# First stage of a three-stage transformer kernel: biases loaded in one piece, TensorE's products regrouped, VectorE's loop unrolled

## The chip, the cores and the metric

The kernel runs on one NeuronCore of a Trainium2 chip. The metric is device time in microseconds of one execution; before the change the median of three runs is 1351.59 us (1350.39 to 1354.27). One more execution was profiled, and its trace is what the rows below come from.

## The reference

Images of 64 x 3 x 128 x 128 are cut into 64 patches of 768 numbers. A first block mixes over the batch with weights of its own for each patch n, a linear chain of five products follows, then a recurrent attention layer and a feed-forward layer. The change touches only the first block:

```python
flat = x.reshape(64, 3, 8, 16, 8, 16).transpose(0, 2, 4, 1, 3, 5).reshape(64, 64, 768)
q = einsum('bnf,nfd->bnd', flat, Wq) + bq        # Wq, Wk, Wv: (64, 768, 192); bq, bk, bv: (64, 192)
k = einsum('bnf,nfd->bnd', flat, Wk) + bk
v = einsum('bnf,nfd->bnd', flat, Wv) + bv
scores = einsum('bnd,cnd->nbc', q, k) / sqrt(192)
attn = einsum('nbc,cnd->bnd', softmax(scores), v)
att = layernorm(attn) * ln_g + ln_b + flat @ p1_w + p1_b
h = chain(att) + att @ p2_w + p2_b               # chain: w0..w4 with biases, linear
h = softmax(h, axis=2)
h = h + attention(layernorm(h)); h = h + ffn(layernorm(h))
```

## The kernel before

Everything is fp32. The five products of the chain and p2 are linear, so the kernel first multiplies them into one 192 x 192 matrix and a bias (`weff`); that is the opening, 0 to about 68 us, TensorE work on `bt` and `chain_w`. Then comes the **first stage**: 32 pairs of patches, one pair per step. For a pair, 128 partitions hold 64 batch rows of each of two patches. A step costs three weight loads of 1152 KB each (Wq, Wk, Wv of two patches) and one of 384 KB (x). The second stage (from about 440 us on) is the recurrent attention and the feed-forward part; no line of it is touched.

Each engine has a program of its own, written out by hand, and the engines meet by semaphores; so the order of the lines in a `step_b` of each engine is the order in which the engine works. A step s works on three pairs at once: `t` = s is new (its products with the weights), `a` = s - 1 is in the middle (scores and softmax), `c2` = s - 2 is old (attention times v, layer norm, projection, softmax). On **TensorE** (`pe`) the pieces of a step have these names below:

- **qk**: `qk_chunk` 0 to 5, 12 products of 64 columns of the array by 384; two products on the two halves of the array run side by side.
- **v**: `v_chunk`, 12 products of 64 columns by 192. **p1**: `p1_chunk`, 6 products of 128 columns by 192.
- **tqk**: four transposes of q and k of pair a. **scores**: four small products of 64 columns.
- **pt**: the transpose of the softmax of pair a. **attn**: its product with v.
- **attT**: two transposes of `att` of pair c2. **proj**: two products with `weff`.

An fp32 product is two records in the trace. Before the change the order is: qk 0-1, tqk, qk 2-5, scores, attT, v 0-2, proj, v 3-5, p1 0-2, pt, p1 3-5, attn. ScalarE copies results out of PSUM: q and k (L832), `attT` (L838, L840), the two exponentials of the scores (L851), that of the last softmax (L857), pt into `probsT` (L863), v (L868). VectorE adds the biases (L1212 for bv, L1224 for bq and bk), makes the layer norm with GpSimd's power between (L1215 to L1238), the maxima (L1241, L1248) and the last scaling (L1262). In steps 2 to 5 VectorE also centres and splits the weights of the second stage (`centre_weights`, `split_weights`), in order behind its own part of the step.

**SyncE** issues all DMAs, in one queue. `load_pair(t)` waits until the buffers of pair t - 2 are free: Wq and Wk for `qk_mm`, Wv for `v_mm`, x for `qkv_done` (p1 done). `load_biases` issues three small DMAs for each pair: 3 KB of bq and bk, and twice 48 KB of bv, each row of bv repeated over 64 partitions. TensorE's step t waits for all four loads of its pair (`wx_in`, 64 counts) before its first qk.

Of the kernel before, what the change touches and what calls it, by code (L numbers as in the profile page):

```python
# [19 lines left out]
ALU = mybir.AluOpType  # L20
# [38 lines left out]
 bias_in0 bias_in1 h_out0 h_out1 qkv_done qk_mm v_mm qk_copied v_copied tqk_mm qkT_ready scores_mm rmax_ready  # L59
# [44 lines left out]
def build(nc, d, out):  # L104

    with ExitStack() as ctx:
# [75 lines left out]
        qk_bias = [part("first", HALF, 2, 4) for _ in range(2)]  # L182
        bv = [part("first", P, ATT) for _ in range(2)]
# [25 lines left out]

        bt = [part("first", P, HC, ATT + 1) for _ in range(2)]  # L210
# [80 lines left out]
        def _(sp):  # L291
# [9 lines left out]
                     (p1w[:, :, :], d["p1_w"])]  # L301
# [39 lines left out]
            load_biases(Step(0, 0))  # L341
# [12 lines left out]

            def step_b(it, u):
                t = Step(it, u)
                if t.inside(PAIRS):
                    load_pair(t)
                t = Step(it, u, 1)
                if t.inside(PAIRS):  # L360
                    load_biases(t)
                c2 = Step(it, u, 4)
                if c2.after(0):
                    store_h(c2)
# [71 lines left out]
        def _(pe):  # L436
# [30 lines left out]
            pe.wait_ge(S["par_in"], 20 * 16)  # L467
# [12 lines left out]
            def step_b(it, u):  # L480
                t, a, c2 = Step(it, u), Step(it, u, 1), Step(it, u, 2)
                new, mid, old = t.inside(PAIRS), a.inside(PAIRS), c2.inside(PAIRS)

                def qk_chunk(c_):
                    for e in range(2):
                        last = mm(PS[64 * e:64 * e + 64, 0, 0:2 * ATT], xt[t.par][:, c_, 64 * e:64 * e + 64],
                                  wt[t.par][:, e, 0:2, c_, :], c_ == 0, c_ == CH - 1)
                    if c_ == CH - 1:
                        last.then_inc(S["qk_mm"], 1)

                def v_chunk(c_):
                    for e in range(2):
                        last = mm(PS[64 * e:64 * e + 64, 1 + t.par, 0:ATT], xt[t.par][:, c_, 64 * e:64 * e + 64],
                                  wt[t.par][:, e, 2, c_, :], c_ == 0, c_ == CH - 1)
                    if c_ == CH - 1:
                        last.then_inc(S["v_mm"], 1)

                def p1_chunk(c_):
                    last = mm(PS[:, 1 + t.par, ATT:2 * ATT], xt[t.par][:, c_, :], p1w[:, c_, :], c_ == 0, c_ == CH - 1)
                    if c_ == CH - 1:  # L500
                        last.then_inc(S["qkv_done"], 1)

                if new:
                    pe.wait_ge(S[f"wx_in{t.par}"], (t.half + 1) * 64)
                    if t.after(1):
                        pe.wait_ge(S["qk_copied"], t.n)
                    qk_chunk(0)
                    qk_chunk(1)
                if mid:
                    pe.wait_ge(S["qk_copied"], a.n + 1)  # L510
                    if a.after(1):
                        pe.wait_ge(S["qkT_ready"], a.n)
                    for k in range(4):
                        last = nc.tensor.transpose(PS[0:HALF, 3, k * P:(k + 1) * P], qk[:, k * HALF:(k + 1) * HALF], ident)  # L514
                    last.then_inc(S["tqk_mm"], 1)
                if new:
                    for c_ in range(2, CH):
                        qk_chunk(c_)
                if mid:
                    pe.wait_ge(S["qkT_ready"], a.n + 1)  # L520
                    if a.after(1):
                        pe.wait_ge(S["expP_ready"], 2 * a.n)
                    for e in range(2):
                        for k in range(2):
                            last = mm(PS[64 * e:64 * e + 64, 4, 0:64], qkT[:, k, 64 * e:64 * e + 64],
                                      qkT[:, 2 + k, 64 * e:64 * e + 64], k == 0, k == 1)
                    last.then_inc(S["scores_mm"], 1)
                if old:
                    pe.wait_ge(S["att_ready"], c2.n + 1)
                    if c2.after(1):  # L530
                        pe.wait_ge(S["zexp_ready"], c2.n)
                    nc.tensor.transpose(PS[0:HALF, 7, 0:P], att[:, 0:HALF], ident)  # L532
                    nc.tensor.transpose(PS[0:HALF, 7, P:2 * P], att[:, HALF:ATT], ident).then_inc(S["attT_mm"], 1)
                if new:
                    if t.after(2):
                        pe.wait_ge(S["v_copied"], t.n - 1)
                        pe.wait_ge(S["att_ready"], t.n - 1)
                    for c_ in range(3):
                        v_chunk(c_)
                if old:  # L540
                    pe.wait_ge(S["attT_copied"], 2 * c2.n + 2)
                    mm(PS[:, 7, 2 * P:2 * P + ATT], attT1[:, :], weff1[:, :], True, False)
                    mm(PS[:, 7, 2 * P:2 * P + ATT], attT2[:, :], weff2[:, :], False, True).then_inc(S["proj_mm"], 1)
                if new:
                    for c_ in range(3, CH):
                        v_chunk(c_)
                    for c_ in range(3):
                        p1_chunk(c_)
                if mid:
                    pe.wait_ge(S["expP_ready"], 2 * a.n + 2)  # L550
                    if a.after(1):
                        pe.wait_ge(S["pt_copied"], a.n)
                    nc.tensor.transpose(PS[:, 5, 0:P], probs[:, :], ident).then_inc(S["pt_mm"], 1)
                if new:
                    for c_ in range(3, CH):
                        p1_chunk(c_)
                if mid:
                    pe.wait_ge(S["pt_copied"], a.n + 1)
                    pe.wait_ge(S["v_copied"], a.n + 1)
                    if a.after(1):  # L560
                        pe.wait_ge(S["attn_ready"], a.n)
                    mm(PS[:, 6, 0:ATT], probsT[:, :], v[a.par][:, :]).then_inc(S["attn_mm"], 1)
# [258 lines left out]
        def _(act):  # L821
            act.wait_ge(S["par_in"], 20 * 16)
# [3 lines left out]
            def step_b(it, u):  # L826
                t, a, c2 = Step(it, u), Step(it, u, 1), Step(it, u, 2)
                if t.inside(PAIRS):
                    act.wait_ge(S["qk_mm"], t.n + 1)
                    if t.after(1):  # L830
                        act.wait_ge(S["tqk_mm"], t.n)
                    act.activation(qk[:, :], PS[:, 0, 0:2 * ATT], ACT.Copy).then_inc(S["qk_copied"], 1)  # L832
                if c2.inside(PAIRS):
# [25 lines left out]
                if a.inside(PAIRS):  # L859
# [3 lines left out]
                    act.activation(probsT[:, :], PS[:, 5, 0:P], ACT.Copy).then_inc(S["pt_copied"], 1)  # L863
                if t.inside(PAIRS):
                    act.wait_ge(S["qkv_done"], t.n + 1)
                    if t.after(2):
                        act.wait_ge(S["attn_mm"], t.n - 1)
                    act.activation(v[t.par][:, :], PS[:, 1 + t.par, 0:ATT], ACT.Copy).then_inc(S["v_copied"], 1)  # L868
# [263 lines left out]
        def _(dve):  # L1132
            dve.wait_ge(S["par_in"], 20 * 16)
# [70 lines left out]
            def step_b(it, u):  # L1204
                a, c2 = Step(it, u, 1), Step(it, u, 2)
                mid, old = a.inside(PAIRS), c2.inside(PAIRS)
                if old:

                    dve.wait_ge(S["attn_mm"], c2.n + 1)
                    dve.wait_ge(S[f"bias_in{c2.par}"], (c2.half + 1) * 48)  # L1210
                    dve.wait_ge(S["prec_ready"], c2.n + 1)
                    dve.scalar_tensor_tensor(out=attn[:, :], in0=PS[:, 6, 0:ATT], scalar=prob_rec[:, :], in1=bv[c2.par][:, :],  # L1212
# [6 lines left out]
                if mid:  # L1219
                    dve.wait_ge(S["tqk_mm"], a.n + 1)  # L1220
                    dve.wait_ge(S[f"bias_in{a.par}"], (a.half + 1) * 48)
                    if a.after(1):
# [3 lines left out]
                                      qk_bias[a.par].rearrange("p e k -> p k e").unsqueeze(3).to_broadcast([HALF, 4, 2, 64]),  # L1226
                                      ALU.add).then_inc(S["qkT_ready"], 1)
                if old:
# [9 lines left out]
                    dve.tensor_tensor(att[:, :], PS[:, 1 + c2.par, ATT:2 * ATT], bhatg[:, :], ALU.add).then_inc(S["att_ready"], 1)  # L1238
# [31 lines left out]
            pipeline(dve, PAIRS, 4, step_b_and_weights)  # L1270
# [258 lines left out]
def host_layout(i):  # L1529
# [10 lines left out]
    d["bqk"] = np.concatenate([halves(a["tok_bq"]), halves(a["tok_bk"])], axis=2).transpose(0, 3, 1, 2)  # L1540
    d["bv"] = a["tok_bv"].reshape(PAIRS, 2, 1, ATT)
# [51 lines left out]
```

## Time and profile before

| | us |
|---|---|
| median of three runs | 1351.59 |
| profiled execution, whole | 1347.21 |
| its span in the trace | 1345.2 |
| opening (until the first qk) | 67.87 |
| first stage, first qk to last result of VectorE | 67.87 to 437.89 |

The span is what the trace shows from the first instruction to the last; 2.0 us lie around it. Times in rows count from the span's start. In the timelines a row is a run of like instructions: its start, its busy time, the engine, the line, what it writes and reads, how many, and in brackets how long the engine was idle before it and what ended that.

### The profile page before, as it was taken

What the parts mean: (1) busy time and instruction counts of PE and PEld (TensorE: products, weight loads), DVE (VectorE), ACT (ScalarE), POOL (GpSimd) and SP (SyncE); (2) the same over time, 40 slices, a digit from 0 to 9 for tenths busy, and PEclk for the clock granted to TensorE, in tenths of its full rate; (3) what the DMA queues carried; (4) which work ended last, traced back from release to release, by engine and by line L of the source; (5) the groups of instructions that cost most, each with busy time, mean ns of one, the idle gap of its engine ahead of it and who ended that gap; (6) DMA issues with size and microseconds to landing.
All of it is one profiled execution on the core that took longest, in us unless ns stands there. A gap on an engine that the chain in (4) does not pass through costs nothing.

```text
span 1345.2 us, 44929 instructions
## 1 busy us (share of the span) xinstructions
PE 1231.8 (92%) x17572; PEld 988.4 (73%) x17572; DVE 858.4 (64%) x2184; ACT 614.7 (46%) x1539; POOL 542.5 (40%) x689
## 2 busy tenths in 40 slices
PE   5898999999997579999999999999999999999975
PEld 5865666666664468888888888888888887888774
DVE  0137433333333368878887888888788878888762
ACT  0012222222222355656665666656566656665532
POOL 0000000000000356566646665665566466656631
PEclk8999999999998689999999999999999999999987
DMA  9888999999991012112212221221122122211210
GB/s 326 300 327 325 381 379 372 374 375 373 376 376 37 18 22 50 32 37 50 38 35 39 46 38 35 40 47 35 36 45 44 32 38 50 38 35 35 47 32 15
DMA packets 219992, 179.22 MB, mean 133 GB/s; under 512 B 164342, under 2 KB 189881, under 8 KB 219321
## 3 DMA queue, kind: packets, MB, share of 16 engines
q1 hardware_dynamic: 219818, 176.79, 41.2%
q8 instruction: 122, 2.00, 0.6%
q14 instruction: 52, 0.43, 0.1%
HBM read 154.72 MB, written 22.02 MB: 131 GB/s over the span
## 4 chain that ended last, share of the span: by engine, by line
PE 32%; issue 29%; POOL 27%; DVE 6%; SPq 2%; DMA 2%; ACT 1%; POOLq 0%; DVEq 0%; ACTq 0%
PE PS L438 28%; POOL region L1110 9%; POOL region L1093 5%; POOL region L1098 3%; POOL region L1076 2%; POOL region L1104 2%; POOL region L1088 1%; PE PS L514 1%; SPq L308 1%; POOL region L1083 1%; POOL region L1060 1%; SPq L398 1%; PE PS L692 1%; PE PS L532 1%; PE PS L599 1%
## 5 line engine op out<-in xcount | busy, mean ns | idle before, releaser
L438 PE MATMUL PS<-region 64*64 64x64 f32 (+6 forms) x5864 | 351.6, 286 | 19.9 <-DVE region L1158 12.7
L438 PEld LDWEIGHTS PS<-region 64*64 64x64 f32 (+3 forms) x5864 | 230.1, 139 | 114.9 <-issue 105.0
L1110 POOL TENSOR_TENSOR region<-region,powers 128x12 f32<-128x12 f32 x96 | 224.2, 2336 | 7.5
L905 ACT ACTIVATE region<-PS 128x512 f32<-128x512 f32 (+1 forms) x192 | 93.3, 486 | 187.1 <-PE PS L438 187.1
L1039 POOL TENSOR_TENSOR region<-region,powers 128x1 f32<-128x1 f32 x32 | 6.1, 189 | 404.2 <-DVE region L1218 404.2
L692 PEld LDWEIGHTS PS<-region 64*64 64x64 f32 x4608 | 145.6, 138 | 22.9 <-issue 18.9
L692 PE MATMUL PS<-region 64*64 64x64 f32 x4608 | 158.4, 223 | 1.4 <-ACT region L938 1.4
L438 PE MATMUL PS<-cw_hi,xr_hi 128*128 128x512 f32 (+3 forms) x384 | 148.5, 387 | 1.9 <-ACT region L905 1.4
L438 PE MATMUL PS<-cw_lo,xr_hi 128*128 128x512 f32 (+3 forms) x384 | 130.6, 340 | 0.0
L438 PE MATMUL PS<-cw_hi,xr_lo 128*128 128x512 f32 (+3 forms) x384 | 130.2, 339 | 0.0
L1351 DVE TENSOR_TENSOR region<-region 128x768 f32<-128x768 f32 x96 | 102.8, 1072 | 39.2 <-POOL region L1110 38.9
L832 ACT ACTIVATE region<-PS 128x384 f32<-128x384 f32 x32 | 15.7, 491 | 192.5 <-PE PS L438 192.5
L1057 POOL TENSOR_TENSOR region<-region,powers 128x1 f32<-128x1 f32 x32 | 6.1, 190 | 228.5 <-DVE region L1442 228.5
L1340 DVE TENSOR_REDUCE region<-region 128x12 f32<-128x768 f32 x96 | 90.7, 945 | 6.6 <-ACT region L910 6.3
L889 ACT ACTIVATE region<-PS,vecs 128x256 f32<-128x256 f32 (+1 forms) x128 | 75.7, 669 | 41.4 <-PE PS L648 41.3
L682 PE MATMUL PS<-region 64*64 64x64 f32 x3072 | 62.0, 226 | 29.4 <-issue 22.3
L682 PEld LDWEIGHTS PS<-region 64*64 64x64 f32 x3072 | 54.3, 138 | 46.8 <-issue 46.8
L1093 POOL TENSOR_TENSOR region<-region,powers 128x12 f32<-128x12 f32 x32 | 72.9, 2277 | 26.9 <-DVE region L1410 26.8
L438 PEld LDWEIGHTS PS<-cw_hi,xr_hi 128*128 128x128 f32 (+1 forms) x384 | 73.0, 190 | 14.5 <-ACT region L905 2.2
L910 ACT ACTIVATE region<-region 128x768 f32<-128x768 f32 x96 | 81.1, 845 | 2.8
L438 PEld LDWEIGHTS PS<-cw_hi,xr_lo 128*128 128x128 f32 (+1 forms) x384 | 73.0, 190 | 8.9
L438 PEld LDWEIGHTS PS<-cw_lo,xr_hi 128*128 128x128 f32 (+1 forms) x384 | 74.0, 193 | 4.6
(170 smaller groups left out, 2280.0 us busy)
## 6 DMA issues: line engine op xcount, KB each, us to landing
region<-in_Wq SPq DMA_DIRECT2D x32, 1152.0 KB, 6.3
region<-in_Wk SPq DMA_DIRECT2D x32, 1152.0 KB, 8.6
region<-in_Wv SPq DMA_DIRECT2D x32, 1152.0 KB, 7.8
region<-in_x SPq DMA_DIRECT2D x32, 384.0 KB, 7.4
n_scratch<-region SPq DMA_DIRECT2D x64, 192.0 KB, 3.3
region<-h_scratch SPq DMA_DIRECT2D x64, 96.0 KB, 2.0
region<-in_w SPq DMA_DIRECT2D x2, 2304.0 KB, 13.2
region<-i_scratch SPq DMA_DIRECT2D x256, 12.0 KB, 1.8
```

Of the source, the lines that this page charges most:

```text
L438: return nc.tensor.matmul(dst, lhsT, rhs, start=first, stop=last)
L682: done = nc.tensor.matmul(dst(slice(to, to + 64), h), lhsT[rows, h, :], rhs(rows, h), start=h < 2, stop=stop, skip_group_check=True)
L692: done = nc.tensor.matmul(dst(rows, h), eT[rows, h, :], rhs(rows, h), start=start and h == odd, stop=stop, skip_group_check=True)
L889: act.activation(kqT[:, pairs, m, :], PS[:, bank, at:at + n * P].rearrange("p (a b) -> p a b", a=n), ACT.Identity, scale=(lnk_g, lnq_g)[m] ...
L905: act.activation(raw[:, col:col + width], PS[:, PIECE_BANK[i], 0:width], ACT.Copy).then_inc(S["raw_ready"], 1)
L910: act.activation(sq[:, m * KD:(m + 1) * KD], raw[:, m * KD:(m + 1) * KD], ACT.Square, scale=HD ** -0.5).then_inc(S["sq_ready"], 1)
L1076: pool.tensor_tensor(tr[:, 4:5], tr[:, 3:4], root[:, 0:1], ALU.pow).then_inc(S["f_rstd"], 1)
L1093: pool.tensor_tensor(norm[:, 1, :], norm[:, 0, :], square_root[:, 0:HEADS], ALU.pow).then_inc(S["n1"], 1)
L1098: pool.tensor_tensor(nscale[:, :, :], mask_n.unsqueeze(1).to_broadcast([P, HEADS, SEQ]), norm[:, 5, :].unsqueeze(2).to_broadcast([P, HEADS ...
L1110: pool.tensor_tensor(rs[:, cols], rs_var[:, cols], root[:, cols], ALU.pow).then_inc(S["rs_ready"], 1)
L1340: dve.tensor_reduce(ssq[:, m * HEADS:(m + 1) * HEADS], sq.rearrange("p (g d) -> p g d", d=HD) [:, m * HEADS:(m + 1) * HEADS, :], AX, ALU.a ...
L1351: dve.tensor_tensor(dst.rearrange("p (g d) -> p g d", d=HD), raw[:, m * KD:(m + 1) * KD].rearrange("p (g d) -> p g d", d=HD), rs[:, m * HE ...
```

## The change

Three parts. (1) All biases are loaded once. bq and bk of all pairs come in one DMA of 96 partitions among the small parameters. bv of all pairs goes, in two DMAs of 64 partitions by 6144 numbers, over the place of `bt` and `chain_w[0]`, which are the buffers of the opening; SyncE therefore waits for the last product of the opening (`eff_mm`) ahead of them. The three small DMAs for each pair are gone. (2) TensorE's step has a new order: attn of c2, tqk, qk 0-5, v 0-5, attT, scores, p1 0-2, proj, p1 3-5, pt. v has one PSUM bank instead of two, p1 two banks of its own, pt lies in the bank of the scores; ScalarE copies v right behind q and k. (3) VectorE's loop of 34 steps is written out (it was a hardware loop with 8 steps ahead and 4 behind).

```diff
-        qk_bias = [part("first", HALF, 2, 4) for _ in range(2)]
-        bv = [part("first", P, ATT) for _ in range(2)]
+        qk_bias = part("first", HALF, PAIRS, 8)
...
+        bv = region[:, used["first"]:used["first"] + PAIRS * ATT].rearrange("p (m f) -> p m f", m=PAIRS)
         bt = [part("first", P, HC, ATT + 1) for _ in range(2)]
...
-                     (p1w[:, :, :], d["p1_w"])]
+                     (qk_bias[:, :, :], d["bqk"]), (p1w[:, :, :], d["p1_w"])]
...
-            def load_biases(t):
-                if t.after(2):
-                    sp.wait_ge(S["attn_ready"], t.n - 1)
-                    settled(sp)
-                sp.dma_start(qk_bias[t.par][:, :, :], d["bqk"][t.n]).then_inc(S[f"bias_in{t.par}"], 16)
-                for e in range(2):
-                    sp.dma_start(bv[t.par][e * 64:e * 64 + 64, :], d["bv"][t.n, e].to_broadcast([64, ATT]))\
-                      .then_inc(S[f"bias_in{t.par}"], 16)
...
+            sp.wait_ge(S["eff_mm"], 1)
+            settled(sp)
+            for e in range(2):
+                sp.dma_start(bv[64 * e:64 * e + 64, :, :], d["bv"][e].to_broadcast([64, PAIRS, ATT])).then_inc(S["bias_in"], 16)
...
-                if new:
-                    pe.wait_ge(S[f"wx_in{t.par}"], (t.half + 1) * 64)
-                    if t.after(1):
-                        pe.wait_ge(S["qk_copied"], t.n)
-                    qk_chunk(0)
-                    qk_chunk(1)
+                if old:
+                    pe.wait_ge(S["pt_copied"], c2.n + 1)
+                    pe.wait_ge(S["v_copied"], c2.n + 1)
+                    if c2.after(1):
+                        pe.wait_ge(S["attn_ready"], c2.n)
+                    mm(PS[:, 6, 0:ATT], probsT[:, :], v[c2.par][:, :]).then_inc(S["attn_mm"], 1)
...
-            pipeline(dve, PAIRS, 4, step_b_and_weights)
+            for s in range(PAIRS + 2):
+                step_b_and_weights(s // 2, s % 2)
```

How the instructions stand on TensorE: first the end of one step of the loop and the start of the next. L438 is the helper `mm` (L430 after the change); 64x384 is qk, 64x192 is v, `p1w` is p1, L553 (L546) is pt, 128x192 from `region` alone is attn, L514 (L506) is tqk. Before:

```order
L438 MATMUL PS<-region 64x192 x6
L438 MATMUL PS<-p1w,region 128x192 x3
L550 REGISTER_ALU
L553 MATMUL PS<-cst,region 128x128 [waits pt_copied,expP_ready]
L438 MATMUL PS<-p1w,region 128x192 x3
L438 MATMUL PS<-region 128x192 [waits attn_ready,v_copied,pt_copied]
L506 REGISTER_ALU [waits wx_in1]
L438 MATMUL PS<-region 64x384 [waits qk_copied]
```

After the change:

```order
L430 MATMUL PS<-p1w,region 128x192 x3
L545 ISA
L546 MATMUL PS<-cst,region 128x128 [waits expP_ready]
L430 MATMUL PS<-region 128x192 [waits attn_ready,v_copied,pt_copied]
L502 REGISTER_ALU
L506 MATMUL PS<-cst,region 96x128 [waits qkT_ready,qk_copied]
L506 MATMUL PS<-cst,region 96x128 x3
L430 MATMUL PS<-region 64x384 [waits v_copied,qk_copied,wx_in1]
L430 MATMUL PS<-region 64x384 x11
L430 MATMUL PS<-region 64x192 x12
```

The three products of p1 that stood between pt and attn now stand ahead of pt, and attn follows pt with nothing between. The middle of a step, again on TensorE; 64x64 is scores, L532 and L533 (L521, L522) are attT, `weff` is proj. Before:

```order
L438 MATMUL PS<-region 64x384 x8
L522 REGISTER_ALU [waits qkT_ready]
L438 MATMUL PS<-region 64x64 [waits expP_ready]
L438 MATMUL PS<-region 64x64 x3
L531 REGISTER_ALU [waits att_ready]
L532 MATMUL PS<-cst,region 96x128 [waits zexp_ready]
L533 MATMUL PS<-cst,region 96x128
L438 MATMUL PS<-region 64x192 [waits att_ready,v_copied]
L438 MATMUL PS<-region 64x192 x5
L541 ISA
L438 MATMUL PS<-weff,region 128x192 [waits attT_copied]
L438 MATMUL PS<-weff,region 128x192
```

After the change:

```order
L430 MATMUL PS<-region 64x384 x11
L430 MATMUL PS<-region 64x192 x12
L521 MATMUL PS<-cst,region 96x128 [waits zexp_ready,att_ready]
L522 MATMUL PS<-cst,region 96x128
L430 MATMUL PS<-region 64x64 [waits pt_copied,qkT_ready]
L430 MATMUL PS<-region 64x64 x3
L430 MATMUL PS<-p1w,region 128x192 [waits att_ready]
L430 MATMUL PS<-p1w,region 128x192 x2
L430 MATMUL PS<-weff,region 128x192 [waits attT_copied]
L430 MATMUL PS<-weff,region 128x192
L430 MATMUL PS<-p1w,region 128x192 x3
```

The v products stand in one run behind qk, ahead of attT and scores, and proj stands between two runs of p1. The third place is SyncE's queue at the end of the opening, from the last parameters of the second stage to the load of pair 2. Before:

```order
L353 DMA wo<-in_WoT 128x1152
L353 DMA ffn1a<-in_ffn1T 128x128
L353 DMA ffn1b<-in_ffn1T 64x128
L325 DMA region<-in_Wq 128x2x1152 [waits qk_mm]
L325 DMA region<-in_Wk 128x2x1152
L325 DMA region<-in_Wv 128x2x1152 [waits v_mm]
L330 DMA region<-in_x 128x768 [waits qkv_done]
L314 DMA region<-in_bqk 96x8
L316 DMA region<-in_bv 64x192 x2
```

After the change:

```order
L343 DMA ffn1a<-in_ffn1T 128x128
L343 DMA ffn1b<-in_ffn1T 64x128
L348 DMA region<-in_bv 64x6144 [waits eff_mm]
L348 DMA region<-in_bv 64x6144
L316 DMA region<-in_Wq 128x2x1152 [waits qk_mm]
L316 DMA region<-in_Wk 128x2x1152
L316 DMA region<-in_Wv 128x2x1152 [waits v_mm]
L321 DMA region<-in_x 128x768 [waits qkv_done]
```

Ahead of the load of pair 2 there are now two DMAs of 64 partitions by 6144 numbers and the wait for `eff_mm`.

## Rows read from the trace of the kernel before

**Rows 1.** A stretch of the steady first stage: busy times, granted clock, DMA

```profile
core 0: us, PE busy (x) PEld busy (x) DVE busy (x) ACT busy (x) POOL busy (x), PEclk, DMA share, GB/s
...
370.00:403.00 33.00, 33.00 (x244) 21.03 (x241) 12.39 (x43) 8.75 (x33) 2.21 (x6) 1.00 0.99 375
```

**Rows 2.** Timeline of one step of the steady loop

```profile
202.28 0.64 PE L514 MATMUL PS<-cst,region 128*96 128x128 f32 x4
...
203.23 0.14 PEld L438 LDWEIGHTS PS<-region 128*64 128x64 f32 x2 [0.18 <-issue]
203.55 0.14 PEld L438 LDWEIGHTS PS<-region 128*64 128x64 f32 x2 [0.18 <-issue]
...
206.22 1.20 PE L438 MATMUL PS<-region 128*64 128x192 f32 x12
...
207.34 0.92 PE L438 MATMUL PS<-weff,region 96*128 96x192 f32 x4
...
210.40 0.27 PE L553 MATMUL PS<-cst,region 128*128 128x128 f32 x1
...
210.51 1.14 PE L438 MATMUL PS<-p1w,region 128*128 128x192 f32 x6
210.71 0.28 ACT L863 ACTIVATE region<-PS 128x128 f32<-128x128 f32 x1 [1.32 <-PE PS L553]
...
211.49 1.93 PE L438 MATMUL PS<-region 128*128 128x192 f32 x10
...
213.35 0.64 PE L514 MATMUL PS<-cst,region 128*96 128x128 f32 x4
```

**Rows 3.** Timeline of the last steps: an attn that waits for its copy

```profile
428.57 0.27 ACT L863 ACTIVATE region<-PS 128x128 f32<-128x128 f32 x1
...
428.89 0.50 PEld L438 LDWEIGHTS PS<-region 128*128 128x128 f32 x2 [1.42 <-ACT region L863]
```

**Rows 4.** Timeline of step 4: VectorE behind the centring of weights

```profile
94.69 1.36 DVE L1186 TENSOR_SCALAR region<-region 49x2304 f32<-49x2304 f32 x1
...
101.36 0.41 DVE L1212 SCALAR_TENSOR_TENSOR region<-PS,region 128x192 f32<-128x192 f32 x1
...
104.61 0.32 PE L532 MATMUL PS<-cst,region 128*96 128x128 f32 x1 [0.93 <-DVE region L1238]
```

**Rows 5.** TensorE's waits from 85 to 135 us: us in total, times, longest

```profile
PE PS L438 <- DVE region L1224: 2.1, 2, 1.8
PE PS L532 <- DVE region L1238: 1.8, 2, 0.9
```

**Rows 6.** Timeline: last product of the opening, first qk, pair 2

```profile
64.13 0.35 DVE L1161 TENSOR_TENSOR weff<-PS,p2a 96x192 f32<-96x192 f32 x1 [4.31 <-PE PS L438]
...
67.87 6.04 PE L438 MATMUL PS<-region 128*64 128x384 f32 x48 [2.47 <-DVE ffn_bias L1176]
...
72.04 0.38 SPq L325 DMA_DIRECT2D region<-in_Wq  x1
...
85.55 0.20 PEld L438 LDWEIGHTS PS<-region 128*64 128x64 f32 x4 [0.23 <-issue]
```

**Rows 7.** Load of x for pair 2 (issued at 76.1 us)

```profile
DMA to landing us min/median/max: 9.0/9.0/9.0
```

**Rows 8.** Stretches of the opening, columns as in rows 1

```profile
17.00:19.50 2.50, 2.50 (x18) 2.50 (x17) 0.00 (x0) 0.00 (x0) 0.00 (x0) 1.00 0.99 69
53.00:61.00 8.00, 6.25 (x39) 5.97 (x38) 1.53 (x2) 0.00 (x0) 0.00 (x0) 1.00 1.01 189
64.00:72.00 8.00, 5.53 (x37) 3.47 (x37) 3.02 (x10) 0.00 (x0) 0.00 (x0) 1.00 0.04 14
74.00:80.00 6.00, 6.00 (x38) 3.56 (x40) 0.69 (x1) 0.33 (x1) 0.00 (x0) 1.00 1.00 409
```

**Rows 9.** Timeline: TensorE starts again in the opening

```profile
29.69 3.56 PE L438 MATMUL PS<-region 128*128 128x193 f32 x10 [9.24 <-DVE region L1158]
```

**Rows 10.** The stretch around that start, columns as in rows 1

```profile
24.90:35.10 10.20, 5.41 (x17) 5.44 (x18) 2.91 (x11) 0.22 (x1) 0.00 (x0) 0.50 1.03 409
```

More of the change, by code:

```diff
@@ L516, in step_b @@
                 if new:
-                    for c_ in range(2, CH):
-                        qk_chunk(c_)
[L519 to L527, printed above, removed]
+                    pe.wait_ge(S[f"wx_in{t.par}"], (t.half + 1) * 64)
+                    if t.after(1):
+                        pe.wait_ge(S["qk_copied"], t.n)
+                        pe.wait_ge(S["v_copied"], t.n)
+                    for c_ in range(CH):
+                        qk_chunk(c_)
+                    for c_ in range(CH):
+                        v_chunk(c_)
                 if old:
@@ L533, in step_b @@
                     nc.tensor.transpose(PS[0:HALF, 7, P:2 * P], att[:, HALF:ATT], ident).then_inc(S["attT_mm"], 1)
+                if mid:
+                    pe.wait_ge(S["qkT_ready"], a.n + 1)
+                    if a.after(1):
+                        pe.wait_ge(S["pt_copied"], a.n)
+                    for e in range(2):
+                        for k in range(2):
+                            last = mm(PS[64 * e:64 * e + 64, 4, 0:64], qkT[:, k, 64 * e:64 * e + 64],
+                                      qkT[:, 2 + k, 64 * e:64 * e + 64], k == 0, k == 1)
+                    last.then_inc(S["scores_mm"], 1)
                 if new:
                     if t.after(2):
-                        pe.wait_ge(S["v_copied"], t.n - 1)
                         pe.wait_ge(S["att_ready"], t.n - 1)
                     for c_ in range(3):
-                        v_chunk(c_)
+                        p1_chunk(c_)
                 if old:
@@ L550, in step_b @@
                     pe.wait_ge(S["expP_ready"], 2 * a.n + 2)
[L551 to L562, printed above, removed]
+                    nc.tensor.transpose(PS[:, 4, P:2 * P], probs[:, :], ident).then_inc(S["pt_mm"], 1)
             for s in range(2):
@@ L862, in step_b @@
                         act.wait_ge(S["attn_mm"], a.n)
[L863 to L868, printed above, removed]
+                    act.activation(probsT[:, :], PS[:, 4, P:2 * P], ACT.Copy).then_inc(S["pt_copied"], 1)
             pipeline(act, PAIRS, 2, step_b)
@@ L1209, in step_b @@
                     dve.wait_ge(S["attn_mm"], c2.n + 1)
-                    dve.wait_ge(S[f"bias_in{c2.par}"], (c2.half + 1) * 48)
+                    dve.wait_ge(S["bias_in"], 32)
                     dve.wait_ge(S["prec_ready"], c2.n + 1)
-                    dve.scalar_tensor_tensor(out=attn[:, :], in0=PS[:, 6, 0:ATT], scalar=prob_rec[:, :], in1=bv[c2.par][:, :],
+                    dve.scalar_tensor_tensor(out=attn[:, :], in0=PS[:, 6, 0:ATT], scalar=prob_rec[:, :], in1=bv[:, c2.n, :],
                                              op0=ALU.mult, op1=ALU.add).then_inc(S["attn_ready"], 1)
```

31 lines of the change are left out of this document (14 added, 17 removed).

## The prediction

> **What bounds the kernel now.** I looked at stretches of the first stage first, since only that stage is changed. From 134 to 403 us TensorE has no idle time at the full clock, and DMA shows 0.99 of its time busy at 375 GB/s [rows 1]. Two resources seem full, so the question is which one waits. The view of waits names nothing that TensorE waited for between 134 and 403 us, no DMA in particular. DMA runs at 409 GB/s when it has work [rows 8], and a step needs 3.93 MB of weights and x plus some 0.2 MB: 4.1 MB / 409 GB/s = 10.1 us of a step of 213.35 - 202.28 = 11.07 us [rows 2]. So TensorE is the bound in the steady part, and DMA has 1 us to spare in each step. VectorE is busy 12.39 of 33 us [rows 1]: writing its loop out gives nothing by itself.
>
> Two places are not steady. In steps 3 to 5 TensorE waits 2.1 + 1.8 = 3.9 us for VectorE [rows 5], which stands behind the second stage's weights [rows 4]. And the load of pair 2 comes just in time: its x is issued at 76.1 and lands 9.0 us later, at 85.1 [rows 7], and TensorE's first qk of that pair starts at 85.55 [rows 6]. Whatever delays that load by more than about half a microsecond stops TensorE, and nothing makes it up later, since every later step is TensorE's.
>
> **The change part by part.**
>
> *Fewer changes of shape.* The trace gives the pure price of each run. qk: two loads of weights start 0.32 apart (203.23, 203.55), 12 times 3.84 us. A record of p1 takes (211.49 - 210.51) / 6 = 0.163, 12 times 1.95. v is half as wide as qk, 12 x 0.163 = 1.95. attn and proj, 6 x 0.163 = 0.98. Seven transposes at 210.51 - 210.40 = 0.11 make 0.77, the four pairs of scores 0.21 by their width. The sum is 9.70, against 11.07 [rows 2]: 1.37 us go into changes between products on half of the array's columns (64) and those on all of them. There are eight in a step: to tqk and back, scores to attT, attT to v, v to proj and back, v to p1, attn to qk. That is 0.17 each. The v run of 206.22 to 207.34 has 1.12 for six products of 0.163, so 0.14 for one change. The new order has four: tqk to qk, v to attT, attT to scores, scores to p1. It saves four, 0.56 to 0.68 us a step; I take 0.62.
>
> *attn directly behind pt.* Between them lies a trip through ScalarE: pt goes to `probsT` and attn reads it. Before, three products of p1 hid it. Now nothing does. pt starts at 210.40, ScalarE's copy at 210.71 and takes 0.28 [rows 2]; in the last steps a copy ended at 428.84 and attn's weights began to load at 428.89 [rows 3]. From pt's start to attn's that is 0.31 + 0.28 + 0.05 = 0.64, of which 0.11 is pt itself: 0.53 idle. Behind it attn's weights no longer load under a running product; that is a start like one after a change of shape, 0.10. In every second step the wait stands on a register instruction at the loop's head, 0.05 on average. Sum 0.67 us. Is ScalarE free for the copy? The last softmax's exponential follows proj; proj stands six p1 records and pt's trip, about 1.4 us, ahead, about what the maximum, its negation and the exponential need. I count no more for it; if the copy is late, each 0.1 us costs 3 us over the stage.
>
> Net in a steady step 0.67 - 0.62 = +0.05; over 30 steps +1.5 us. The bounds: 0.53 - 0.68 = -0.15 gives -4.5 us, and 0.78 (the trip and 0.1 of a late copy) - 0.56 = +0.22 gives +6.6 us. The last trip stands in the drain, where nothing is saved: +0.5.
>
> *Steps 2 to 5.* VectorE's work on the weights takes 101.36 - 94.69 = 6.67 us in step 2, and 3.25 more pass until attT can start (104.61) [rows 4]. In the new order TensorE has 0.43 (attn) + 0.58 (tqk) + 3.84 + 1.95 = 6.8 us of work between attn and attT. I let VectorE end its own part when attn starts, because its last results hang on proj, which is now 1.4 us ahead of that. Then attT waits 6.67 + 3.25 - 6.8 = 3.1 us, against 1.8 + 0.9 before [rows 5]: +0.4. The three other blocks are shorter; with the same shift of 0.3 each, the four cost +1.3 us. What waits behind attT is all of the rest of the step, so this is on the path.
>
> *v copied earlier, banks, SyncE's small DMAs.* The earlier copy waits for v and is needed a step later; the small DMAs (99 KB a step) relieve DMA, which has spare time, and SyncE. 0 here. If the steps became 1 us shorter, DMA would be next.
>
> *The single load of bv.* This is the term that decides. It is 2 x 64 x 6144 x 4 B = 3.15 MB, as much as was loaded in pieces, but all ahead of pair 2. SyncE issues it when the opening's last product is through, 64.1 [rows 6]. DMA is indeed idle then, 0.04 of 64 to 72 us [rows 8], and the load of pair 2 is issued at 72.04 [rows 6]. With 1.5 us from issue to flow, at 409 GB/s the 3.15 MB would end at 73.3 and hide. But each of the two DMAs goes to one half of the partitions. The same form stands in the trace: from 53 to 61 us the weights of 64 and of 49 partitions flow, DMA is 1.01 busy, and it moves 189 GB/s [rows 8]. At that rate bv takes 16.6 us and ends at 65.7 + 16.6 = 82.3. The Trainium skill says why (SBUF — State Buffer, section "Door 1: The DMA port swizzle"): partitions 0 to 63 reach only 8 of 16 ports, at best about 218 GB/s, and two DMAs to the two halves do not add up. By its figure, which is an estimate from that page, bv takes 14.4 us; the stretch at 189 GB/s agrees with the rule.
>
> The weights of pair 2 stand behind it in the queue. 3.93 MB at 409 GB/s are 9.6 us, and 1 us goes by until the slowest of the queues is through (before: 72.04 + 1.5 to 85.1 is 11.6, with the start from an idle queue). I take a rate between 189 and half of 409, which ends bv at 81.3: x lands at 91.9. TensorE comes to the first qk of pair 2 at 85.55 + 0.67 (trip) + 0.58 (tqk now stands ahead) - 0.2 (changes saved) = 86.6. It idles **5.3 us**; bounds 4.3 and 6.3.
>
> *The clock.* That idle time has a price of its own. In the opening TensorE stopped for 9.24 us up to 29.69 [rows 9], and its granted clock was 0.50, the lower of the two levels (1.2 GHz), from 24.9 to 35.1 [rows 10]: it fell 4.4 us after the engine had stopped and came back 5.4 us after it had started, at a loss of 2.7. An idle time of 5.3 us is near the 4.4; I count half, +1.3.
>
> **Sum.** 1.5 + 0.5 + 1.3 + 5.3 + 1.3 = +9.9 us on the profiled 1347.2, so 1357 for a profiled execution, and 1351.6 + 9.9 = 1361.5, about **1361 us**, for the median, which stood 4.4 above the profiled one. The likeliest case's own range: 1355 to 1368.
>
> **The rivals.**
> - *bv flows at the full rate and hides.* For: engines may drift apart, so that both halves are written at once. Against: 189 GB/s in the like stretch. Then 5.3 and 1.3 fall away, +3.3: 1355 us. Chance 13%.
> - *bv is held up at its source.* All 64 partitions read the same row. For: from 17 to 19.5 us four small loads of one row to 128 partitions flowed, DMA 0.99 busy, 69 GB/s [rows 8]. Against: the pieces in the steady stage do the same and cost no wait. At 69 GB/s bv takes 45.6 us, x of pair 2 lands near 122, TensorE idles 35: 1351.6 + 3.3 + 35 + 2.7 = 1393 us. Chance 12%.
> - *The new order wins.* Place: from pt to attn in each step. If TensorE did not lose the trip (the next run of weights and tqk going on in its shadow), a step would be 11.07 - 0.62 = 10.45, 18.6 us less over 30; with the load of pair 2 late as above, 1351.6 - 18.6 + 8.4 = 1341 us. It decides from a loss under 0.2 us per step on, where the saving pays for the late load too. Against it stands the order: attn is in front of tqk in the same queue. Chance 11%.
>
> **How the numbers follow.** A measurement tells this kernel from no change beyond about 0.3%, 4 us. The likeliest case has 64%, and is slower by more than that in nine of ten; the second rival is slower; the first is mostly within 4 us, the third faster. That makes slower 0.74, the same 0.14, faster 0.12. The range leaves out the second rival and most of the third: 1349 to 1371.
>
> **What the profile would show.** Right: about 65.7 to 81 us at about 200 GB/s; x of pair 2 landing near 92; TensorE idle some 5 us before its third run of qk, at the lower clock for a few us behind it; a steady step of 11.0 to 11.2 us with one idle time of about 0.5 us, ended by L851, in each. Wrong: a step under 10.8 (the trip is not lost), bv done by 74 (full rate) or after 90 (source), or a wait of attn much over 0.6 us, which would mean that ScalarE is not free and would move the result up by 3 us for each 0.1.

## The result

The kernel after the change takes **1359.39 us** (median of 7 executions, 1354.75 to 1363.51), the kernel before, timed beside it, 1350.39 (7 executions, 1346.89 to 1354.27). The ratio is **1.0073**, its 95% interval 1.0056 to 1.009: slower by 7.6 to 12.2 us. The prediction had 1361, a range of 1349 to 1371, and slower at 0.74. In two of the experiments below one execution lay far off (2355.40 us in e3, 3701.27 in e11) and is left out of the ratio.

The two profiled executions lie further apart than the medians, 1360.7 against 1345.2 us of span. Where these 15.5 us arise:

| place | before | after | after is behind by |
|---|---|---|---|
| first qk of pair 0 | 67.87 | 67.62 | -0.25 |
| first qk of pair 2 | 85.55 | 91.46 | 5.9 |
| tqk of the last pair | 422.03 | 433.10 | 11.1 |
| first product of the second stage | 446.30 | 458.44 | 12.1 |
| end of the span | 1345.2 | 1360.7 | 15.5 |

The last 3.4 us arise in the second stage, whose code is the same (granted clock 0.97 before, 0.96 after, over that stretch), and are no part of the change. The first 5.9 are the place that the prediction named. By the issue of x for pair 5 the kernel is 10.2 behind (110.61 before, 120.76 after), and from there to the last pair only 1 us is added. TensorE's timeline of the changed kernel there (columns as in [rows 2]):

```profile
86.17 0.27 PE L546 MATMUL PS<-cst,region 128*128 128x128 f32 x1
86.90 0.59 PE L430 MATMUL PS<-region 128*128 128x192 f32 x2 [0.45 <-ACT region L851]
87.32 0.60 PE L506 MATMUL PS<-cst,region 128*96 128x128 f32 x4
91.46 0.91 PE L430 MATMUL PS<-region 128*64 128x384 f32 x2 [3.54 <-DMA region<-in_x]
```

The last row is the first qk of pair 2, with 3.54 us of idle time ended by x. [rows 6] show 85.55 for it (its weights' load) and no wait. SyncE's queue of the same kernel shows why x is late:

```profile
63.92 1.11 SPq L348 DMA_DIRECT2D region<-in_bv  x2
73.48 0.39 SPq L316 DMA_DIRECT2D region<-in_Wq  x1
...
77.58 0.34 SPq L321 DMA_DIRECT2D region<-in_x  x1
```

and the views of the lines L348 (both DMAs of bv) and L321 (x of pair 2) give the times from issue to landing:

```profile
L348 SPq DMA_DIRECT2D region<-in_bv x2: 471/534/597, 63.9 to 64.4; - x2
...
DMA to landing us min/median/max: 9.7/13.1/16.6
...
L321 SPq DMA_DIRECT2D region<-in_x x1: 340/340/340, 77.6 to 77.6; - x1
...
DMA to landing us min/median/max: 13.8/13.8/13.8
```

bv is issued at 63.9 and 64.4 and lands at 73.6 and 81.0; x of pair 2 lands at 77.6 + 13.8 = 91.4, where [rows 7] have 9.0 us for it. Stretches of the changed kernel (columns as in [rows 1]):

```profile
66.00:72.00 6.00, 4.38 (x18) 2.20 (x20) 1.30 (x5) 0.00 (x0) 0.00 (x0) 0.75 0.96 197
74.00:80.00 6.00, 6.00 (x48) 4.43 (x45) 0.69 (x1) 0.33 (x1) 0.00 (x0) 1.00 0.93 189
91.00:98.00 7.00, 6.54 (x28) 2.74 (x30) 0.00 (x0) 0.03 (x1) 0.00 (x0) 0.62 1.02 421
113.50:120.00 6.50, 5.93 (x25) 5.46 (x26) 1.44 (x7) 1.93 (x8) 0.00 (x0) 0.50 0.92 376
370.00:403.00 33.00, 31.82 (x245) 21.83 (x243) 12.19 (x43) 9.06 (x33) 2.21 (x6) 1.00 0.96 363
```

While bv flows, DMA is 0.93 to 0.96 busy and moves 189 to 197 GB/s, half of the 409 that [rows 8] have for weights: 3.15 MB at 193 GB/s are 16.3 us. Behind the idle time the granted clock is at the lower level (0.50, 1.2 GHz) for most of 91 to 98 (0.62 on average), and once more from 113.5 to 120 (0.50). In a view of TensorE alone qk and v of pair 2 are one row, and it takes 8.40 us where the like row of pair 0 has 6.04 in [rows 6]:

```profile
91.46 8.40 PE L430 MATMUL PS<-region 128*64 128x384 f32 x48 [3.54 <-DMA region<-in_x]
```

In the steady stretch TensorE, which had 33.00 of 33 us in [rows 1], has 31.82: there is now an idle time in each step. TensorE's waits from 62 to 145 us, and from 145 to 405 (columns as in [rows 5]):

```profile
PE PS L521 <- DVE region L1220: 4.8, 2, 3.2
PE PS L430 <- DMA region<-in_x: 3.5, 1, 3.5
...
PE PS L430 <- ACT region L851: 2.1, 5, 0.5
...
PE PS L430 <- ACT region L851: 9.8, 24, 0.4
```

One steady step of TensorE and of ScalarE's copy:

```profile
210.83 0.27 PE L546 MATMUL PS<-cst,region 128*128 128x128 f32 x1
211.55 0.59 PE L430 MATMUL PS<-region 128*128 128x192 f32 x2 [0.45 <-ACT region L851]
...
221.93 0.27 PE L546 MATMUL PS<-cst,region 128*128 128x128 f32 x1
...
211.14 0.28 ACT L851 ACTIVATE region<-PS 128x128 f32<-128x128 f32 x1
```

pt starts at 210.83, the copy at 211.14, attn at 211.55: the trip takes 0.72 us, and 0.45 of it show as idle (0.64 and 0.37 in every second step). Yet the step is no longer than before: SyncE issues x alternately 11.01 and 11.11 us apart, 11.06 on average, against 11.07 [rows 2].

### The profile page after: what moved, and what is told of

It is laid out like the page before. It is cut to its first block, busy times and chain, and to the rows that moved or that the text cites. A ratio compares the mean times of both kernels' runs of the same rounds, so it can differ in the third digit from the quotient of the medians.

```text
span 1360.7 us, 44475 instructions
## 1 busy us (share of the span) xinstructions
PE 1230.5 (90%) x17572; PEld 1003.1 (74%) x17572; DVE 857.5 (63%) x2184; ACT 618.2 (45%) x1539; POOL 542.4 (40%) x689
## 4 chain that ended last, share of the span: by engine, by line
issue 31%; POOL 28%; PE 27%; DVE 7%; DMA 3%; SPq 2%; ACT 2%; POOLq 0%; DVEq 0%; ACTq 0%
PE PS L430 24%; POOL region L1093 9%; POOL region L1076 5%; POOL region L1081 3%; POOL region L1087 2%; POOL region L1059 2%; POOL region L1071 1%; POOL region L1043 1%; SPq L308 1%; POOL region L1066 1%; DMA region<-in_x 1%; DVE region L1230 1%; PE PS L506 1%; PE PS L521 1%; ACT region L851 1%
## 5 line engine op out<-in xcount | busy, mean ns | idle before, releaser
L430 PE MATMUL PS<-region 64*64 64x64 f32 (+6 forms) x5864 | 346.5, 287 | 32.3 <-ACT region L851 13.7
L430 PEld LDWEIGHTS PS<-region 64*64 64x64 f32 (+3 forms) x5864 | 235.1, 140 | 137.1 <-issue 114.3
L430 PE MATMUL PS<-cw_hi,xr_hi 128*128 128x512 f32 (+3 forms) x384 | 149.5, 389 | 1.9 <-ACT region L888 1.4
L430 PE MATMUL PS<-cw_lo,xr_hi 128*128 128x512 f32 (+3 forms) x384 | 131.6, 343 | 0.0
L430 PE MATMUL PS<-cw_hi,xr_lo 128*128 128x512 f32 (+3 forms) x384 | 131.5, 343 | 0.0
L430 PEld LDWEIGHTS PS<-cw_hi,xr_hi 128*128 128x128 f32 (+1 forms) x384 | 73.7, 192 | 14.6 <-ACT region L888 2.2
L1223 DVE TENSOR_REDUCE region<-PS 128x1 f32<-128x64 f32 x32 | 7.2, 225 | 120.3 <-PE PS L430 120.3
L430 PEld LDWEIGHTS PS<-cw_hi,xr_lo 128*128 128x128 f32 (+1 forms) x384 | 73.8, 192 | 9.0
```

What stands on the lines that cost most here:

```text
L430: return nc.tensor.matmul(dst, lhsT, rhs, start=first, stop=last)
```

## The experiments

The theory: two costs, the late load of pair 2 and the trip from pt to attn, and one saving, the fewer changes of shape, which cancels the trip. The rivals: the loss lies in TensorE's order alone; bv is slow at its source and not at the halves; the changes of shape cost nothing. All ratios are to the kernel before, timed on the same chip; "step" is the mean distance between two issues of x in the steady part.

| run | median us | ratio, 95% interval | step | idle before pair 2 |
|---|---|---|---|---|
| after | 1359.39 | 1.0073, 1.0056 to 1.009 | 11.06 | 3.5 |
| e1 biases and loop, old order | 1355.56 | 1.0036, 1.0021 to 1.005 | 11.07 | 4.8 |
| e2 bv in one DMA, 2 x 64 | 1414.70 | 1.0467, 1.0445 to 1.0488 | 11.06 | 59.8 |
| e3 bv with its pair | 1352.72 | 1.0015, 1.0 to 1.0029 | 11.06 | 0 |
| e4 tqk in front of attn | 1347.65 | 0.998, 0.9967 to 0.9993 | 10.62 | 6.2 |
| e5 before, trip exposed | 1368.47 | 1.0121, 1.0099 to 1.0143 | 11.72 | 0 |
| e6 e3 and e4 | 1342.10 | 0.993, 0.9906 to 0.9954 | 10.62 | 0.6 |
| e7 bv row by row, 128 | 1351.88 | 1.0003, 0.9989 to 1.0018 | 11.06 | 0 |
| e8 bv row by row, 2 x 64 | 1357.99 | 1.0052, 1.0033 to 1.0072 | 11.06 | 4.6 |
| e9 e6, VectorE's pieces spread | 1330.61 | 0.9876, 0.9856 to 0.9896 | 10.62 | 0.5 |
| e10 e9, pt earlier | 1326.72 | 0.9844, 0.9824 to 0.9864 | 10.52 | 0.7 |
| e11 VectorE's loop alone | 1350.40 | 1.0006, 0.9993 to 1.0018 | 11.06 | 0 |
| e12 e10, bv as in e7 | 1327.20 | 0.9823, 0.9803 to 0.9842 | 10.52 | 0 |

**e1, parts 1 and 3 without part 2.** The kernel after the change with TensorE's and ScalarE's steps, and the banks, of before.

> The single load of the biases and VectorE's loop written out, with the order of TensorE and ScalarE from before the change. My theory (the load of bv keeps pair 2 late, the new order is worth nothing net): bv ends near 81 us, x of pair 2 lands near 91.5, and TensorE, which comes there at about 85.5, idles 5.5 to 6; with some lower clock behind it the kernel takes +7 to +8 us over before, 1357 to 1358. Rival (the loss lies in TensorE's new order, and the late load is made up): +0 to +3 us, 1350 to 1353.

It takes 0.36% more, 4.9 us (2.8 to 6.7). x lands at 90.7 and TensorE idles 4.79 us before pair 2. The new order isn't needed for that loss. By its time alone the rival (at most +3) isn't quite out; the 4.79 us of idle time, which it did not allow, rule it out. The size is 2 to 3 us under the expectation, and the runs don't say why.

**e11, part 3 alone.**

```diff
-            pipeline(dve, PAIRS, 4, step_b_and_weights)
+            for s in range(PAIRS + 2):
+                step_b_and_weights(s // 2, s % 2)
```

> The kernel before the change with VectorE's loop written out, and nothing else. My theory: VectorE has idle time in every step, so nothing changes: within 1.5 us of before, steady step 11.06. Rival (the loop's head on VectorE is on the path of the waits for attT): up to 2 us less.

No difference that can be measured, and the same step.

**e3, bv with its pair.** `load_bv` stands between Wv and x, and counts on the pair's own semaphore:

```diff
-            for e in range(2):
-                sp.dma_start(bv[64 * e:64 * e + 64, :, :], d["bv"][e].to_broadcast([64, PAIRS, ATT])).then_inc(S["bias_in"], 16)
+            for n in range(2):
+                load_bv(Step(0, n), "bias_in")
...
+                if t.after(2):
+                    load_bv(t, f"wx_in{t.par}")
```

> The kernel after the change, with bv of pairs 0 and 1 alone behind the opening, and that of each later pair (two DMAs of 64 partitions by 192 numbers) between the weights and x of its own pair. My theory: pair 2 is in time, x lands at about 85.5, no idle time of TensorE there and no lower clock behind it, 6 to 8 us less than after the change: 1352, with a steady step of 11.06 as after. Rival (the new order costs the time): it stays within 2 us of 1359.

As expected: no idle time before pair 2, and 0.58% of 1350, 7.8 us, are back. What is left, 1.0015 (1.0 to 1.0029), is the price of part 2 and of the loop written out: 2 us, not clear of nothing, where the prediction's terms for it made 3.3.

**e7 and e8, halves or source.** In both, bv lies in memory once for each partition; e7 brings it in one DMA of 128 partitions, e8 in two of 64. The edits of the load, e7's and then e8's:

```diff
-            for e in range(2):
-                sp.dma_start(bv[64 * e:64 * e + 64, :, :], d["bv"][e].to_broadcast([64, PAIRS, ATT])).then_inc(S["bias_in"], 16)
+            sp.dma_start(bv[:, :, :], d["bv"]).then_inc(S["bias_in"], 16)
...
-                sp.dma_start(bv[64 * e:64 * e + 64, :, :], d["bv"][e].to_broadcast([64, PAIRS, ATT])).then_inc(S["bias_in"], 16)
+                sp.dma_start(bv[64 * e:64 * e + 64, :, :], d["bv"][64 * e:64 * e + 64]).then_inc(S["bias_in"], 16)
```

> The kernel after the change; bv is laid out in memory once for each partition, and one DMA of 128 partitions by 6144 numbers brings it. Theory of the halves (two DMAs that each write 64 partitions flow at half of the rate): about 400 GB/s, a packet of 24 KB takes 0.9 to 1.0 us and not 1.93, bv is through by 74.5, x of pair 2 lands by 86.5, 6 us less than after the change: 1353. Theory of the source (the row that 64 partitions share is slow to read): the same, since here no row is shared. This run tells neither from the other by itself, but with the next.

> As the run before, with a row in memory for each partition, but in two DMAs of 64 partitions each. Theory of the halves: a packet takes 1.93 us as in the kernel after the change, bv ends near 81 us, the time stays near 1359. Theory of the source: a packet takes 0.9 to 1.0 us, bv is through by 74.5, 1353.

The same stretch, from 66 to 72 us, in e7 and then in e8:

```profile
66.00:72.00 6.00, 3.83 (x24) 2.13 (x26) 1.77 (x7) 0.00 (x0) 0.00 (x0) 1.00 0.93 396
...
66.00:72.00 6.00, 5.57 (x24) 2.81 (x26) 0.17 (x1) 0.00 (x0) 0.00 (x0) 0.72 0.93 197
```

DMA is busy 0.93 in both, and moves 396 GB/s to all partitions, 197 to the halves. A packet of 24 KB takes 0.91 us in e7 and 1.91 in e8 (medians of the 128 packets in each trace), as the theory of the halves had it. No row is shared in either, so the source isn't the cause. bv is through at 75.5 and at 82.3, x of pair 2 lands at 85.3 and 91.3, and the kernels differ by 0.49%, 6.6 us. This is what the Trainium skill says (SBUF — State Buffer, section "Can I just issue two DMAs to hit both halves?"): two DMAs to the two halves serialize, and only one transfer over all 128 partitions reaches every port. The runs agree, 197 against 396 GB/s.

**e2, one DMA with the shared rows.** Meant as the same test without the copies in memory:

```diff
-            for e in range(2):
-                sp.dma_start(bv[64 * e:64 * e + 64, :, :], d["bv"][e].to_broadcast([64, PAIRS, ATT])).then_inc(S["bias_in"], 16)
+            sp.dma_start(bv[:, :, :], bass.AP(d["bv"].tensor, 0, [[PAIRS * ATT, 2], [0, 64], [ATT, PAIRS], [1, ATT]])).then_inc(S["bias_in"], 16)
```

> The kernel after the change, with bv as one DMA to all 128 partitions in place of two to 64 each. My theory (half of the partitions take the data at half of the rate): it flows at about 400 GB/s, is through by 74 us, x of pair 2 lands at 85 to 86.5, TensorE's idle time of 3.5 us before its third run of qk is gone, and the kernel takes 6 to 8 us less than after the change: about 1352. Rival (the one source row that 64 partitions read holds it up): the same row is read as often, so bv still ends near 81 us and the time stays near 1359.

Neither came: 63 us slower than before. A stretch of it, and TensorE at pair 2:

```profile
106.00:112.00 6.00, 0.00 (x0) 0.00 (x0) 0.00 (x0) 0.00 (x0) 0.00 (x0) 0.50 0.12 53
...
146.14 4.11 PE L429 MATMUL PS<-region 128*64 128x384 f32 x12 [59.84 <-DMA region<-in_x]
```

DMA's mean share is 0.12 while all else waits: 2 of 16 engines, each at the full 53 / 2 = 26 GB/s (409 / 16 = 25.6). The source's outermost dimension has two entries. The Trainium skill has that rule (DMA: Bandwidth & Descriptors, section "Why a DMA increments its semaphore by 16 and not by 1"): the number of engines is the largest up to 16 that divides the outermost dimensions of both sides, here 2. The share of 0.12 agrees. So this run doesn't tell halves from source by its time; e7 and e8 do. (Its packets of 24 KB take 0.91 us, as in e7, although the row is shared.)

**e4, tqk in front of attn.** The two pieces change places at the head of TensorE's step, bv stays late.

> The kernel after the change, with tqk in front of attn, so that the trip from pt through ScalarE to attn lies in tqk's shadow; bv stays as it is. My theory (the order saves about 0.6 us a step in changes of shape, and the trip eats it): the idle time of 0.4 us before attn is gone, a steady step takes 10.5 to 10.65 in place of 11.06, 12 to 16 us less in all, about 1345. Rival A (the changes of shape cost nothing, and the trip was hidden by something else before): the step stays within 0.1 of 11.06 and the time within 3 us of 1359. Rival B (DMA is next): the step falls to no less than 10.8 and TensorE shows waits for x.

12.6 us less than after the change (1.0073 - 0.998). TensorE in e4, pt, tqk, attn, and the next pt:

```profile
210.22 0.27 PE L546 MATMUL PS<-cst,region 128*128 128x128 f32 x1
210.33 0.60 PE L500 MATMUL PS<-cst,region 128*96 128x128 f32 x4
210.94 6.56 PE L430 MATMUL PS<-region 128*128 128x192 f32 x50
...
220.88 0.27 PE L546 MATMUL PS<-cst,region 128*128 128x128 f32 x1
```

No idle time shows before attn, and the step is 10.66 and 10.57 alternately. The new order does save time, which the trip had eaten; rival A falls, and B too, since no steady step waits for x. At pair 2 TensorE is early and idles 6.2 us.

**e5, the trip alone.** The kernel before, with pt behind all of p1:

```diff
+                if new:
+                    for c_ in range(3, CH):
+                        p1_chunk(c_)
                 if mid:
                     pe.wait_ge(S["expP_ready"], 2 * a.n + 2)
...
-                if new:
-                    for c_ in range(3, CH):
-                        p1_chunk(c_)
```

> The kernel before the change, with one edit of TensorE's order: pt stands behind all six products of p1, so that attn follows it with nothing between. No change of shape is saved or added. My theory (the trip through ScalarE costs what the new order saves, about 0.44 us a step, by the step of 11.06 with and 10.62 without the trip): a steady step of 11.5, an idle time of 0.4 to 0.5 before each attn, ended by ScalarE, +13 to +16 us over before, about 1364. The same theory with the sizes of the prediction (0.67 a step): 11.7 and +20 us. Rival (the idle time before attn is free, because TensorE's time then comes back elsewhere): step 11.1, at most +3 us.

16.4 us slower (13.4 to 19.3). TensorE in e5, around one attn, and the same transposes of a later step:

```profile
200.12 0.31 PE L532 MATMUL PS<-cst,region 128*96 128x128 f32 x1
...
205.62 0.27 PE L556 MATMUL PS<-cst,region 128*128 128x128 f32 x1
206.26 2.07 PE L438 MATMUL PS<-region 128*128 128x192 f32 x10 [0.37 <-ACT region L863]
208.27 0.64 PE L514 MATMUL PS<-cst,region 128*96 128x128 f32 x4
...
211.85 0.31 PE L532 MATMUL PS<-cst,region 128*96 128x128 f32 x1
```

The step is 211.85 - 200.12 = 11.73 (the mean 11.72): the trip costs 0.65 us, although only 0.37 shows as idle. From pt's start to attn's are 0.64, where the next product came 0.11 behind pt before ([rows 2]): 0.53 more. attn and the four products of qk behind it take 2.01 until tqk (206.26 to 208.27), where [rows 2] have 1.86 (211.49 to 213.35): 0.15 more. In the trace attn's weights begin to load at 206.26, as attn does, and no longer under a running product; that the 0.15 is theirs is read from this and not tested. The size of the step is the prediction's 0.67, not the 0.44 that e4 seemed to say: e4 had hidden two thirds of the trip. The whole, 16.4, stays under the +20 of that size.

**e6, e9, e10: the two repairs together, and what was next.** e6 is e3 with e4. e9 spreads VectorE's work on the second stage's weights, one instruction (twice two) in each of nine steps:

```diff
-                if s.known and 2 <= s.n < 6:
-                    (centre_weights, split_weights)[s.n % 2]((s.n - 2) // 2)
+                if 2 <= s.n < 11:
+                    weight_piece(s.n - 2)
```

e10 puts pt one product of p1 earlier:

```diff
                 if new:
-                    for c_ in range(3, CH):
+                    for c_ in range(3, CH - 1):
                         p1_chunk(c_)
                 if mid:
                     pe.wait_ge(S["expP_ready"], 2 * a.n + 2)
                     nc.tensor.transpose(PS[:, 4, P:2 * P], probs[:, :], ident).then_inc(S["pt_mm"], 1)
+                if new:
+                    p1_chunk(CH - 1)
```

> tqk in front of attn, and bv of each pair loaded with its own pair. If the two costs add (6.7 us for the late load in the new order, 11.7 for the trip): 1347.7 - 6.7 = 1341, perhaps 1 to 2 less, since the quicker TensorE waited 6.2 us for pair 2 where it had been 3.5; steady step 10.6. Rival (DMA is now the bound, with a need of 10.1 us a step, and the small loads of bv are in its way): the step is 10.8 or more, waits for x show in the steady steps, and the time is 1345 or more.

> tqk in front of attn, bv with its pair, and VectorE's nine pieces of work on the second stage's weights spread over steps 2 to 10, one in each, in place of four blocks in steps 2 to 5. My theory: the waits of attT for VectorE (6.3 us in all from 62 to 145 us) and the lower clock behind them are gone, 6 to 8 us less than with the blocks: 1342.1 - 7 = 1335. Rival (each piece of up to 2.8 us is longer than VectorE's idle time between two steps, about 2.7, and pushes attT back): 9 waits of 0.1 to 0.5 us, a gain of only 2 to 4 us.

> As the run before, with pt one product of p1 earlier, so that attn's weights load under a running product too. The step with tqk alone in the trip's shadow is 10.62 where the saving of the changes of shape (0.65, from 11.06 + 0.65 - 11.06) would allow 11.06 - 0.65 = 10.41. My theory (0.2 of the trip is left in the exposed load of attn's weights): the steady step falls to 10.4, 5 to 6 us less than the run before. Rival A (DMA, with a need of 10.1 us a step, is in reach): 10.5 or more with waits for x. Rival B (the exponentials of the scores end too late for the earlier pt): an idle time before pt, no gain.

e6: 1342.1, as the sum of the two said. e9: 1330.6, 11.5 under e6 (compared by ratios, 0.54%, 7.3 us); the expected 7. All of TensorE's waits from 62 to 145 us in e6, then in e10:

```profile
PE PS L528 <- DVE region L1227: 6.3, 3, 3.6
PE PS L437 <- DVE ffn_bias L1166: 2.6, 1, 2.6
PE PS L437 <- DMA region<-in_x: 0.6, 1, 0.6
...
PE PS L437 <- DVE ffn_bias L1168: 2.5, 1, 2.5
PE PS L437 <- DMA region<-in_x: 0.7, 1, 0.7
```

The waits of attT for VectorE are gone, in e9's trace as in e10's. e10's pt to the next pt:

```profile
201.36 0.27 PE L553 MATMUL PS<-cst,region 128*128 128x128 f32 x1
...
211.84 0.27 PE L553 MATMUL PS<-cst,region 128*128 128x128 f32 x1
```

10.48 (and 10.55 alternately), 10.52 on average and not 10.4: half of what e4 had left. TensorE waits for nothing from 145 to 385 us, so neither rival is seen, and where the other 0.1 goes stays open. The medians of e10 and e9 are 3.9 us apart; the ratios' intervals overlap, so the total alone doesn't prove it, the step does. **e10 beats both kernels**: the one before by 1.56%, the one after the change by 2.3% (0.9844 / 1.0073).

**e12, does DMA hold the step?** e10 with bv as in e7.

> As the version with pt one product earlier and VectorE's pieces spread, with bv in one DMA of 128 partitions behind the opening (a row in memory for each partition) in place of two small DMAs for each pair. DMA moves 389 to 409 GB/s in that version, near the most seen. My theory (TensorE sets the step, x lands 1.5 us or more before it is needed): the steady step stays at 10.52, the time within 2 us of 1326.7. Rival (the small DMAs of 64 partitions, 98 KB at 190 GB/s or 0.5 us of DMA in each step, slow the step): 10.4, 3 us less.

The step stays at 10.52 and the time within what can be told from e10's. DMA isn't what sets the step, at 389 GB/s (280 to 340 us) to 409 (350 to 380) in e10.

## Why the prediction was right

- **The total.** +9.9 was forecast, and 0.73% of 1350 is 9.9. So close a hit is luck: the terms below are off by up to 3 us each, in both directions.
- **The load of bv** carries the result. With what was measured in brackets: issue 64.1 (63.9), end 81.3 (81.0), rate about 200 GB/s (189 to 197), x of pair 2 at 91.9 (91.4): right, and its cause is shown by e7 against e8. The term of 5.3 + 1.3 = 6.6 us is 6.6 by e8 - e7 (0.49%), 7.8 by after - e3, 9.4 by after - e7; in the old order e1 has 5.
- **Its split was off.** The idle time was 3.5 in the profiled execution, since TensorE arrived at 87.9 and not at 86.6. qk and v of pair 0 took 7.73 us where [rows 6] have 6.04, 1.7 more, at the lower clock (0.75 from 66 to 72). Without them TensorE would have come at 86.2 and idled 5.2, an estimate from these rows; so the 5.3 was right for an execution without that stretch. The 5.9 us of the table are thus 3.5 of waiting, 1.7 of lower clock and 0.9 for attn, its trip and tqk, which now stand ahead of the qk, less 0.25 at the start. e1, e8 and e4 idle 4.8, 4.6 and 6.2. The clock behind it cost more than the 1.3 counted: from 91 to 98 the granted clock averages 0.62, so (1 - 0.62) x 7 = 2.7 us are lost, of which 0.2 fall in idle time; the row of 8.40 us for 6.04 says 2.4.
- **The saving** of 0.62 us a step: e5 - before gives 0.65 for the trip, the step after the change is equal to that before, so the saving is 0.65 as well, if the trip costs the same in both orders, which no run shows; 0.54 (11.06 - 10.52, e10) is measured outright. That it comes from the changes of shape is read from the trace, since no run varies them alone. The kernel before, and then the kernel after:

```profile
207.34 0.92 PE L438 MATMUL PS<-weff,region 96*128 96x192 f32 x4
208.19 1.20 PE L438 MATMUL PS<-region 128*64 128x192 f32 x12
209.32 1.24 PE L438 MATMUL PS<-p1w,region 128*128 128x192 f32 x6
...
220.30 0.82 PE L430 MATMUL PS<-weff,region 96*128 96x192 f32 x4
220.95 1.14 PE L430 MATMUL PS<-p1w,region 128*128 128x192 f32 x6
```

  proj between two runs of v takes 0.85 us from start to start, between two of p1 0.65. v and proj together take 3.10 (206.22 to 209.32), and 12 x 0.163 + 0.65 = 2.61 by the prices without a change: 0.49 for three changes, 0.16 each, as four for 0.65.
- **The trip**, 0.67, is 0.65. **The net** +0.05 was 0.00, so the +1.5 us over the stage did not come; e3's 1.0015 and e7's 1.0003 for all of part 2 (3.3 predicted, 2.0 and 0.4 measured, with intervals of some 2 us) agree.
- **Steps 2 to 5**, +1.3: in waits 4.8 against 3.9 us, +0.9. But the longest, 3.2, has the lower clock behind it (113.5 to 120, TensorE 5.93 busy at 0.50, up to 3.0 us), which the prediction did not count. It does not come in the traces of before and e5; e11, in the old order too, has it (granted 0.82 from 106 to 121), so it is no price of the new order alone.
- **The drain**, +0.5: from tqk of the last pair to the second stage 25.34 against 24.27, +1.1. attT is waited for 3.21 us with the scores now queued behind it.
- **The rivals.** Full rate: no, 197 GB/s. Held up at the source: no, e8 without any shared row is as slow. The new order wins: no as it stands, since attn heads the queue; e4 shows that one exchange of two pieces is all it lacked, and there 0.44 us a step come, of the 0.62 that the rival counted; with pt one product earlier (e10) 0.54.

## What to carry to other kernels

A large load split over two halves of the partitions flows at half of the rate (197 GB/s against 396 here), and DMA's busy share doesn't show it (0.93 in both): judge "it fits into the idle time" by the rate of that form, and look at what is queued behind it. When products are regrouped, the piece that had covered a trip through another engine must be replaced by some other piece of no dependence (here tqk, and one p1), and the gain is read off the step with the trip exposed alone. A stall in a stage that TensorE bounds can cost more than its length, through the clock behind it: here 3.5 us of waiting and 2.4 more.

## What the hardware showed unexpectedly

A DMA whose source has two entries in its outermost dimension ran on 2 of 16 engines: share 0.12, 53 GB/s, 60 us of idle time (e2).

The lower clock after pauses is not the same in each execution. The first qk in e9, and then in the kernel after the change:

```profile
68.11 6.04 PE L437 MATMUL PS<-region 128*64 128x384 f32 x48 [2.48 <-DVE ffn_bias L1166]
...
67.62 7.73 PE L430 MATMUL PS<-region 128*64 128x384 f32 x48 [2.47 <-DVE ffn_bias L1159]
```

TensorE's pause of 2.5 us before the first qk is in every profile; the run of qk behind it took 6.04 us in before, e2, e4, e7, e9 and e12, and 7.73 in after, e1, e3, e5, e6, e8, e10 and e11. Neither the biases nor the order divides the two lists. The first qk's own start does: 67.69 to 68.17 us in the first list, 66.28 to 67.62 in the second. Why stays open, so 1.7 us come and go by something that no run here sets. It also widens the difference of two profiled executions beyond that of the medians.

An idle time of 0.37 us in the profile cost 0.65 us of step (e5): what shows as idle was only part of what the trip cost.
